# Two stacked products in place of three for the low-rank terms of the first network

## The reference

```python
gate   = x @ W_gate + (x @ sA_gate @ sB_gate) / 8 + sum_e w[e] * (x @ A_gate[e] @ B_gate[e]) / 8
up     = x @ W_up   + (x @ sA_up   @ sB_up  ) / 8 + sum_e w[e] * (x @ A_up[e]   @ B_up[e]  ) / 8
hidden = silu(gate) * up                        # 688 columns
out    = hidden @ W_down + (the same two low-rank terms of hidden)
x      = layernorm(x + out)
```

## Time and profile before

| | |
|---|---|
| Median of 3 runs | 1401.04 us (1400.85 to 1401.22) |
| The profiled execution: its own time | 1409.79 us |
| The profiled execution: span | 1408.0 us |
| Mean granted clock of TensorE | 0.984 of full speed |
| TensorE busy (matmul) | 1350.0 us, 96% of the span |
| VectorE, ScalarE, GpSimd busy | 993.7, 611.3, 566.9 us |

### The profile page before, as it was taken

One profiled execution on the slowest core, in us unless ns is written; L12 is line 12 of the kernel. 1 busy time (PEld: TensorE's weight loads), 2 busy tenths in 40 slices (PEclk: granted clock), 3 DMA queues, 4 the chain that ended last, 5 costly groups with the idle time before them and its releaser, 6 DMA issues.

```text
span 1408.0 us, 24791 instructions
## 1 busy us (share of the span) xinstructions
PE 1350.0 (96%) x8292; PEld 1108.4 (79%) x8292; DVE 993.7 (71%) x2519; ACT 611.3 (43%) x1497; POOL 566.9 (40%) x466
## 2 busy tenths in 40 slices
PE   8999999999999999899999999999999999985995
PEld 7788888888888888788887888888888888863664
DVE  5788888888888888865454565765765666874226
ACT  4555555555555555642323333433433434441332
POOL 3776656565656565802104232222222212313222
PEclk9999999999999999999999999999999999987998
DMA  6000000000000200120000200200200002777994
GB/s 190 1 12 1 13 0 11 0 11 0 11 0 11 66 0 1 21 70 1 0 1 0 76 8 16 76 9 16 75 8 15 8 9 53 203 260 227 282 266 135
DMA packets 67952, 76.16 MB, mean 54 GB/s; under 512 B 14189, under 2 KB 55173, under 8 KB 67877
## 3 DMA queue, kind: packets, MB, share of 16 engines
q1 hardware_dynamic: 56533, 58.36, 14.3%
q10 hardware_dynamic: 8560, 12.36, 3.0%
q0 software_dynamic: 2784, 4.46, 1.6%
HBM read 66.22 MB, written 8.95 MB: 53 GB/s over the span
## 4 chain that ended last, share of the span: by engine, by line
PE 83%; DVE 6%; ACT 4%; issue 3%; DMA 2%; another core or an unknown queue 1%; POOL 0%; SPq 0%; DVEq 0%; ACTq 0%; POOLq 0%
PE ps L1857 43%; PE ps L2003 9%; PE ps L1958 6%; PE ps L2040 4%; PE ps L1964 2%; PE ps L2225 2%; PE ps L1978 2%; PE ps L1974 2%; PE ps L1975 2%; DMA wo<-in_L_attn_wo_dram 1%; PE ps L2215 1%; PE ps L2452 1%; PE ps L2138 1%; PE ps L2374 1%; PE ps L2139 1%
## 5 line engine op out<-in xcount | busy, mean ns | idle before, releaser
L860 ACT ACTIVATE probs<-ps,nm 128x128 f32<-128x128 f32 (+3 forms) x256 | 135.4, 529 | 198.7 <-DVE nm L1277 198.7
L717 POOL TENSOR_TENSOR qk<-q,ksb 128x512 f32<-128x512 f32 x64 | 85.7, 1340 | 306.2 <-ACT q L978 214.6
L2003 PE MATMUL ps<-kT,qT 128*128 128x128 f32 (+3 forms) x512 | 159.3, 434 | 3.2 <-ACT probs L860 3.2
L1209 DVE TENSOR_TENSOR prod<-ps,rope_sb 128x1024 f32<-128x1024 f32 x128 | 155.5, 1217 | 7.3 <-PE ps L1857 7.3
L557 POOL TENSOR_TENSOR qT<-prod 64x512 f32<-64x512 f32 x64 | 82.0, 1281 | 140.5 <-DVE prod L1209 133.3
L1187 DVE TENSOR_TENSOR pT_low<-ps,pT 128x384 fp32r<-128x384 f32 (+2 forms) x256 | 104.8, 451 | 44.4 <-ACT pT L794 44.4
L1277 DVE CUSTOM_DVE_ANT_0 ps<-ps,causal 128x128 f32<-128x128 f32 (+3 forms) x256 | 122.7, 500 | 3.1 <-PE ps L2003 3.0
L557 POOL TENSOR_TENSOR kT<-prod 64x512 f32<-64x512 f32 x64 | 82.1, 1282 | 70.2 <-DVE prod L1209 64.8
L1857 PEld LDWEIGHTS ps<-kvo,qn 128*128 128x128 f32 x768 | 100.8, 192 | 8.6 <-DVE qn L1187 3.9
L1331 DVE SCALAR_TENSOR_TENSOR acc<-ps,rinv,acc 128x256 f32<-128x256 f32 x256 | 106.0, 476 | 2.1 <-issue 2.1
L794 ACT ACTIVATE pT<-ps 128x384 fp32r<-128x384 f32 (+2 forms) x256 | 84.9, 415 | 51.4 <-PE ps L2040 51.3
(11 more groups left out here) (303 smaller groups left out, 3046.9 us busy)
## 6 DMA issues: line engine op xcount, KB each, us to landing
eg<-in_L_ffn_w_gate_dram SPq DMA_DIRECT2D x16, 704.0 KB
eg<-in_L_ffn_w_up_dram SPq DMA_DIRECT2D x16, 704.0 KB
ed<-in_L_ffn_w_down_dram ACTq DMA_DIRECT2D x10, 640.0 KB
ksb<-ks_dram SPq DMA_DIRECT2D x16, 256.0 KB, 3.3
ed<-in_L_ffn_w_down_dram SPq DMA_DIRECT2D x6, 640.0 KB
rows_dram<-rows ACTq DMA_DIRECT2D x4, 640.0 KB, 7.7
acc<-in_L_attn_x_dram SPq DMA_DIRECT2D x4, 512.0 KB
wq_in<-in_L_attn_wq_dram SPq DMA_DIRECT2D x8, 256.0 KB, 2.9
```

The lines of the kernel that those rows point to most:

```text
L717: nc.gpsimd.tensor_tensor(qk[:], q3[:], ksb[b % 2][:], ALU.mult).then_inc(qk_ready, 1)
L860: nc.scalar.activation(probs[hh][:, off:off + (i + 1) * P], ps[:, BS + i % 2, 0:(i + 1) * P], ACT.Exp, bias=nm[:, hh, i:i + 1], scale=-1.0 ...
L1209: nc.vector.tensor_tensor(prod[parity][w][:], ps[:, BA:BA + 2, :], rope[:, w:w + 1, :].broadcast_to([P, 2, T]), ALU.mult).then_inc(product ...
L2003: pe.matmul(ps[:, bank, 0:(i + 1) * P], qT[:, hh, b, i * P:(i + 1) * P], kT[:, hh, b, 0:(i + 1) * P], start=True, stop=True).then_inc(scor ...
```

## The change

The three products of `lora` become two. `lb_wide` has 128 rows: the rounded `lb` of rows 0 to 63 twice; against it `xaT_wide` has the rounded activations of rows 0 to 63 and below them their rests. `lb_rest` has 104 rows: the rests of all 72 rows, rounded ones of rows 64 to 71 in between or behind, with `xaT_rest` to match: its rows 0 to 63 the rounded activations, 64 to 71 and 72 to 79 those of the last expert (72 to 79 a second copy that `route0` writes to `xa`), 80 to 95 zero, 96 to 103 the rests of the last expert. Partitions of `lb_in` from 72 to 103 are loaded with the last expert's matrix again, 4 times for gate and 4 for up.

```diff
+NX, NB = 80, 104
-        lb_in = place("lb_in", 137, [NL, 2, F0])
+        lb_in = place("lb_in", 137, [NB, 2, F0])
-        lb = [place(f"lb{h}", 42 + 5.5 * h, [NL, 2, F0], F32R) for h in range(2)]
+        lb_wide = place("lb_wide", 42, [P, 2, F0], F32R)
+        lb_rest = place("lb_rest", 47.5, [NB, 2, F0], F32R)
-        xaT = [place(f"xaT{h}", 56 + 12 * h, [NL, 2, T], F32R) for h in range(2)]
+        xaT_wide = place("xaT_wide", 68, [P, 2, T], F32R)
+        xaT_rest = place("xaT_rest", 56, [NB, 2, T], F32R)
-        xa = place("xa", 90, [P, TPB, 2 * NL])
+        xa = place("xa", 90, [P, TPB, 2 * NX])
-        w0_pieces.append(([h[:] for h in lb], lb_in[:]))
+        w0_pieces.append(([lb_wide[0:64], lb_rest[0:64]], lb_in[0:64]))
@@ SyncE, load_small
                     sp.dma_start(lb_in[R0:NL, w, :], io["L0_ffn_B_" + name].rearrange("e r n -> (e r) n")).then_inc(lb_loaded, 16)
+                    for at in range(NL, NB, R0):
+                        sp.dma_start(lb_in[at:at + R0, w, :], io["L0_ffn_B_" + name][E0 - 1]).then_inc(lb_loaded, 16)
@@ GpSimd, the pieces
-                    pool.wait_ge(lb_loaded, 64)
+                    pool.wait_ge(lb_loaded, 192)
...
+            one = ones[64:NB, :].rearrange("p (a n) -> p a n", a=1).broadcast_to([NB - 64, 2, F0])
+            nc.gpsimd.tensor_tensor(lb_rest[64:NB], lb_in[64:NB], one, ALU.mult).then_inc(w0_hi, 1)
+            nc.gpsimd.memset(xaT_rest[64:96].bitcast(F32), 0.0)
+            pool.wait_ge(w0_hi, w0_first + 7)
             pool.wait_ge(w0_lo, w0_first + 6)
+            nc.gpsimd.tensor_tensor(lb_rest[64:NL], lb_in[64:NL], lb_rest[64:NL].bitcast(F32), ALU.subtract).then_inc(w0_lo, 1)
+            pool.wait_ge(w0_lo, w0_first + 7)
@@ ScalarE, xa_halves
-                    copy(xaT[0][:, w, :], ps[0:NL, xa_bank(b) + w, :]).then_inc(xahi_ready, 1)
+                    copy(xaT_wide[0:64, w, :], ps[0:64, xa_bank(b) + w, :])
+                    copy(xaT_rest[0:NX, w, :], ps[0:NX, xa_bank(b) + w, :]).then_inc(xahi_ready, 1)
@@ ScalarE, before xa_halves(0)
+            act.wait_ge(w0_lo, w0_first + 7)
+            copy(lb_wide[64:P], lb_in[0:64])
@@ VectorE, route0
+                for k in range(2):
+                    nc.vector.tensor_tensor(
+                        xa[:, 2 * k:2 * k + 2, :].rearrange("p i (w c) -> p i w c", w=2)[:, :, :, NL:NX],
...
@@ VectorE, xa_rests
-                    rest(xaT[1][:, w, :], ps[0:NL, xa_bank(b) + w, :], xaT[0][:, w, :]).then_inc(xalo_ready, 1)
+                    rest(xaT_wide[64:P, w, :], ps[0:64, xa_bank(b) + w, :], xaT_rest[0:64, w, :])
+                    rest(xaT_rest[96:NB, w, :], ps[64:NL, xa_bank(b) + w, :], xaT_rest[64:NL, w, :]).then_inc(xalo_ready, 1)
@@ TensorE, turn_xa
-                        last = pe.transpose(ps[0:NL, xa_bank(b) + w, i * P:(i + 1) * P], xa[:, i, w * NL:(w + 1) * NL], ident[:])
+                        last = pe.transpose(ps[0:NX, xa_bank(b) + w, i * P:(i + 1) * P], xa[:, i, w * NX:(w + 1) * NX], ident[:])
@@ TensorE, lora
-                    last = mm3(ps[0:size, 2 * w + m % 2, :], lambda a: lb[a][:, w, f:f + size],
-                               lambda c: xaT[c][:, w, :], False, True)
+                    pe.matmul(ps[0:size, 2 * w + m % 2, :], lb_wide[:, w, f:f + size], xaT_wide[:, w, :], start=False, stop=False)
+                    last = pe.matmul(ps[0:size, 2 * w + m % 2, :], lb_rest[:, w, f:f + size], xaT_rest[:, w, :],
+                                     start=False, stop=True)
@@ TensorE, after turn_xa(0)
-            pe.wait_ge(w0_lo, w0_first + 6)
+            pe.wait_ge(w0_lo, w0_first + 7)
```

More of the change, by code:

```diff
@@ L254, in program @@
         w0_hi, w0_lo, w0_first = wd_hi, wd_lo, 1
-        dn_hi, dn_lo, dn_first = wd_hi, wd_lo, 7
+        dn_hi, dn_lo, dn_first = wd_hi, wd_lo, 8
         olo_ready, olo_first = x_turned, KD * BATCH
@@ L312, in program @@
         e_loaded = x_in + [gu_loaded, lb_loaded]
-        e_loaded_first = (16, 16, 16, 16, 32, 64)
+        e_loaded_first = (16, 16, 16, 16, 32, 192)
         rows_stored = [sem("rows_stored"), rope_loaded, la_loaded, dn_loaded]
@@ L1390, in route0 @@
                 settle()
+                for k in range(2):
+                    nc.vector.tensor_tensor(
+                        xa[:, 2 * k:2 * k + 2, :].rearrange("p i (w c) -> p i w c", w=2)[:, :, :, NL:NX],
+                        ps[:, bank + k, 0:2 * NA].rearrange("p (i c) -> p i c", i=2)[:, :, E0:NA].rearrange(
+                            "p i (w c) -> p i w c", w=2)[:, :, :, NL - R0:NL],
+                        wnext[:, 2 * k:2 * k + 2, E0:E0 + 1].rearrange("p i (a e) -> p i a e", a=1).broadcast_to([P, 2, 2, R0]),
+                        ALU.mult)
                 for i in range(TPB):
@@ L1393, in route0 @@
                     nc.vector.tensor_tensor(
-                        xa[:, i, :].rearrange("p (w e r) -> p w e r", w=2, r=R0),
+                        xa[:, i, :].rearrange("p (w c) -> p w c", w=2)[:, :, 0:NL].rearrange("p w (e r) -> p w e r", r=R0),
                         ps[:, bank + i // 2, (i % 2) * NA + E0:(i % 2 + 1) * NA].rearrange("p (w e r) -> p w e r", w=2, r=R0),
```

## The result

| | before | changed |
|---|---|---|
| Median | 1400.85 us (9 runs) | 1404.74 us (9 runs) |
| Ratio | | 1.0035 [1.0024, 1.0045] |
| Profiled execution, span | 1408.0 us | 1403.0 us |
| Low-rank to the next stage, in it | 183.31 us | 187.16 us |

The account below looks back on a forecast made before the run. The prediction took TensorE, busy 96% of the span, as the bound, except at batch starts. It summed +2.4 (batch 0) + 5.1 (batches 1 to 3) - 7.4 (products) = +0.1, giving 1401.2 us, range 1398.8 to 1404.5.

Parts of the forecast that it names:

- Products: Low-rank products per tile, six to four: 11.1 us gross; tiles 2 to 5 keep 7.4, tiles 0 and 1 nothing at turns.
- Halves and rests: Start of batches 1 to 3: more copies and rests of `xaT` ahead of VectorE's adds, 5.1 us in all.
- D: Delay of tile 2 per batch start: 1.70 us, from +0.50 for the later copy and 1.20 for two more rests.
- Everything behind it has its old length: Start of batches 1 to 3: the chain behind the delayed rests keeps its length, so tile 2 starts 1.70 us late.
- rival 1: TensorE's clock falls at the starts of batches 1 to 3: +6 us over three batches, 1407 us; chance 0.05.
- busy stretches of 5.8 us between the stands: Batch starts: TensorE's dense work between its two stands, put forward as evidence against the clock falling.
- the stand of 2.16 us in the earlier trace: TensorE's stand in the kernel before, through which the granted clock held 1.00; cited on the lower clock.
- the forecast stand of 1.7: Batches 1 to 3: TensorE stands 1.7 us for VectorE's adds, then again 1.6 before tile 2.
- Start-up, +2.4: Batch 0: eight more loads delay GpSimd's list, TensorE waits for it, and tile 2 starts 2.4 us later.
- hidden by GpSimd: Batch 0: VectorE's two added `route0` operations, 0.2 us each, end at 608.0, before GpSimd is done at 609.65.
- GpSimd's neighbour: Start-up: GpSimd's new 6.6 us beside VectorE's `route0` could become 9.3, 2.7 us more; the sum leaves this out.
- Sum: +2.4 for batch 0, +5.1 for batches 1 to 3, -7.4 for products: +0.1 us, giving 1401.2 us.

Follow-up runs that it names:

- The reordered rests: Changed kernel with both rests of `xaT_wide` first, then both of `xaT_rest`, the first waiting for the last copy; ratio to the kernel before 1.0065.
- the stand filled: Changed kernel with 20 unused transposes ahead of the first base product of batches 1 to 3; ratio to the kernel before 1.0031.
- the shorter stand (1.11): Changed kernel without the rests of the last expert's eight rows of activations, part of the result missing; ratio to the kernel before 1.0013.
- undoing them: Changed kernel with loads last, GpSimd's subtraction deferred, TensorE's wait for it later, and rests split around statistics and normalization at turns; 1391.65 us, ratio 0.9943.
- the kernel before with the split: Kernel before with adds and statistics first at a turn, rests of w=0 during GpSimd's root, w=1 behind normalization; 1396.48 us on the same chip.

## Why the prediction was wrong, step by step

*Products: right.* Tiles 2 to 5 keep their gain, -7.34 against -7.4, and tiles 0 and 1 bring nothing at the turns. Rows cost nothing: starts 0.23 to 0.24 apart with 128 rows as with 104.

*Halves and rests, D = 1.70: mis-sized.* D is 2.10, outside the bounds of 0.9 to 1.7. The delay of the first rest is as forecast (1.58 behind `haT` instead of 1.11), but I took 0.60 for every rest from a pair that lies on the same partitions, and these alternate between two sets of partitions, 0.70 to 0.72 apart. Four of them take 2.84 up to the adds where two took 1.21. Three turns: +1.2 us over the forecast. The Trainium skill, "VectorE: DVE Perf Modes", section "Two Vector instructions with no wait between them", has a model for it: an instruction is held until all earlier ones have finished when its operands start in another quadrant than the last ones did. The reordered rests agree, 0.60 inside a pair and 0.70 between pairs.

*"Everything behind it has its old length": the step that failed most.* The 24 base products behind the adds took 8.62, 7.37 and 7.36 us instead of 5.81, at a granted clock down to 0.50, and so became the chain themselves. That is rival 1, which had a chance of 0.05. I set against it busy stretches of 5.8 us between the stands, and that the stand of 2.16 us in the earlier trace rows kept the clock. That row was luck: the same stand lost it in ten of 17 traces, the changed kernel's among them. The larger D also made 2.26 us of the forecast stand of 1.7. The last sentence of the prediction on this rival, that short stands between dense work need not lose the clock, holds here for 1.11 us and not for 2.26. It cost 2.6 us over three turns, not 6, as the longer products first use up slack: with the stand filled, `gated` starts 1.1 us after the low-rank products that it needs. So 2.8 us more in the products became 1.7 at one turn, and 1.56 became 0.4 at the other two. The filled stand and the shorter stand (1.11) show the cause; how long a stand ahead of these products may be, no run shows between 1.11 and 2.26 us.

*Start-up, +2.4: right size by luck, wrong way.* It came out at +2.31, by another path. Loads 2.6 us in place of 4.4; GpSimd done at 607.85 in place of 609.65; but VectorE's routing, which I had called hidden by GpSimd, was held by it for 2.55 us. Under "GpSimd's neighbour" I asked only whether GpSimd would be slowed, not VectorE, and thought of two SBUF inputs above all; the cast that was held has one. Where the clock falls there as well it is +3.9.

*Sum.* 2.3 + 6.3 + 2.6 - 7.3 = +3.9 us in the profiled pair, +5.3 when run again, 4.9 by the ratio. Of the 3.8 us between forecast and profiled pair, D has 1.2 and the clock 2.6. That these two, and batch 0, are the whole loss is shown by undoing them: the stage came out at 175.80 where 176.0 was worked out ahead. Not all of the 7.3 us is net gain even so. Against the kernel before with the split (181.42) it is 5.6 us: each turn is 0.63 us longer, with TensorE standing 1.28 us for the rests.

## What to carry to other kernels

A saving on the busiest engine is worth only what the places around it leave: list who must prepare the new operands, and put that work where the chain of waits has slack, not ahead of its head. Before new work goes on GpSimd beside VectorE's short operations, look at whether these have two SBUF inputs or copy from SBUF to SBUF, as the cast does; here each such one waited for the end of the GpSimd instruction beside it, unless that was a memset. And price a stand of TensorE at its length and at the clock behind it: let a wait stand as late as the first instruction that needs it.

## What the runs showed of the hardware that I had not expected

VectorE operations of 32 elements took 1.42 to 2.83 us beside GpSimd instructions on 8 to 40 partitions, each to within 0.1 us of the end of the GpSimd instruction it met. An operation with one input in PSUM was not held (0.28 for two), nor was one with two SBUF inputs beside a memset (0.19). TensorE's stand of 2.26 us at a turn was followed by the lower clock all 18 times in six traces, and one of 3.01 all three times; the stand of 2.13 to 2.16 us at 587 us in ten of 17 traces; batch 0's of 2.24 to 2.68 us in four of six. Behind stands of 1.11, 1.28 and 1.57 us in the first network it never fell.
